# Decoder layer, attention stage: small vector operations placed in other quarters of a batch, the counting products in another quarter, and three places instead of two for stacked queries and keys

## What is computed

```python
    x = x + _L0_attn_ref(_layernorm(x, axis=-1), ...)
    x = x + _L0_xattn_ref(_layernorm(x, axis=-1), ctx_768, ...)
    x = x + _L0_ffn_ref(_layernorm(x, axis=-1), L0_ffn_Wr, L0_ffn_W1, L0_ffn_W2)
```

```python
        q = (query @ Wq + bq).reshape(B, Nq, H, D).transpose(0, 2, 1, 3)
        k = (key_value @ Wk + bk).reshape(B, Nkv, H, D).transpose(0, 2, 1, 3)
        v = (key_value @ Wv + bv).reshape(B, Nkv, H, D).transpose(0, 2, 1, 3)
        attn = jnp.einsum('bhqd,bhkd->bhqk', q, k) * scale
        attn = jnp.clip(attn, -CLAMP, CLAMP)
        attn = jax.nn.softmax(attn, axis=-1)
        x = jnp.einsum('bhqk,bhkd->bqhd', attn, v).reshape(B, Nq, Cq)
        return x @ Wo + bo
...
        logits = flat @ Wr.T
        weights, ids = jax.lax.top_k(logits, K)
        weights = jax.nn.softmax(weights, axis=-1)
```

## Time and profile before

| | |
|---|---|
| median of 3 runs | 1611.56 us (1610.73 to 1614.21) |
| the profiled execution, its own time | 1611.83 us |
| its span, first to last instruction | 1609.9 us |
| PE busy in the span | 1367.0 us (85%) |
| DVE busy | 1020.0 us (63%) |
| POOL busy | 786.4 us (49%) |
| ACT busy | 553.0 us (34%) |
| one batch of the attention stage | 22.14 us (28 batches, 560.43 to 1180.40) |
| busy between 900 and 1000 us | PE 90.86, DVE 81.26, POOL 71.31, ACT 48.74 us |
| granted TensorE clock, mean of the span | 0.953 |

### The profile page before, as it was taken

How to read it: one execution, slowest core, us unless ns; L and a number is a source line. 1 busy time by engine, 2 the same in 40 slices (tenths; PEclk the granted TensorE clock), 3 DMA queues, 4 the chain that set the end, 5 groups by cost and what they waited for, 6 DMA issues and landing times. The chain is left out here.

```text
span 1609.9 us, 31655 instructions
## 1 busy us (share of the span) xinstructions
PE 1367.0 (85%) x9914; PEld 947.0 (59%) x9915; DVE 1020.0 (63%) x2361; ACT 553.0 (34%) x1356; POOL 786.4 (49%) x1072
## 2 busy tenths in 40 slices
PE   4788778877746998999998899999986699999996
PEld 2455555545534666666666666666664366666664
DVE  2687987798741777888787888888875122222221
ACT  1333323323311345444354444444442112122221
POOL 3234643463343557766666666777664122222222
PEclk9999999999975899999899999999995799999999
DMA  4992000000005655656555564655551122222222
GB/s 148 304 321 60 1 1 1 0 0 1 1 0 92 93 85 106 117 113 107 109 103 115 109 113 96 111 117 118 112 110 38 39 45 44 46 46 46 44 45 23
DMA packets 180329, 128.01 MB, mean 80 GB/s; under 512 B 69010, under 2 KB 173090, under 8 KB 180194
## 3 DMA queue, kind: packets, MB, share of 16 engines
q1 hardware_dynamic: 167890, 112.23, 33.0%
q0 software_dynamic: 12304, 14.10, 5.8%
HBM read 36.10 MB, written 44.83 MB: 50 GB/s over the span
## 5 line engine op out<-in xcount | busy, mean ns | idle before, releaser
L1327 DVE TENSOR_REDUCE neg_raw<-bank_s 100x2 f32<-100x722 f32 x256 | 231.0, 902 | 97.4 <-PE bank_s L1536 86.5
L1220 ACT ACTIVATE prob<-bank_st 120x400 f32<-120x400 f32 (+1 forms) x384 | 166.3, 512 | 190.1 <-PE bank_st L1553 190.1
L1877 POOL DMA_INDIRECT out<-result,target x57 | 88.2, 1547 | 266.6 <-DVE result L1851 263.7
L1338 DVE TENSOR_SCALAR bank_st<-bank_st 120x400 f32<-120x400 f32 (+1 forms) x384 | 195.3, 570 | 0.2 <-issue 0.2
L748 PE MATMUL bank_l<-q_heads,k 128*100 128x192 f32 (+4 forms) x512 | 119.3, 372 | 65.4 <-DVE attn L562 52.2
L1075 POOL TENSOR_TENSOR neg_diag<-xident_b,neg_max 100x400 bf16<-100x400 bf16 x128 | 109.4, 855 | 124.7 <-DVE neg_max L1332 116.4
L1862 DVE TENSOR_TENSOR hidden<-silu,ebank_v 128x512 f32<-128x512 f32 x57 | 39.2, 688 | 196.7 <-PE ebank_v L1786 196.7
L1536 PE MATMUL bank_s<-k_st,q_st 96*100 96x361 bf16 x512 | 130.6, 337 | 35.0 <-DVE neg_raw L1327 21.4
L748 PEld LDWEIGHTS bank_l<-q_heads,k 128*100 128x100 f32 x512 | 79.0, 172 | 113.8 <-DVE attn L562 43.2
L396 ACT ACTIVATE q_heads<-q 32x192 f32<-32x192 f32 (+3 forms) x168 | 62.1, 370 | 224.4 <-DVE q L521 221.4
L1544 PEld LDWEIGHTS bank_st<-q_st,k_st 96*120 96x120 bf16 (+1 forms) x1536 | 109.9, 137 | 22.2 <-ACT prob L1220 10.9
(11 more groups left out here) (203 smaller groups left out, 2724.7 us busy)
## 6 DMA issues: line engine op xcount, KB each, us to landing
k_st<-k_part SPq DMA_DIRECT2D x384, 90.2 KB
slot_rows<-empty SPq DMA_DIRECT2D x9, 2967.0 KB, 26.3
q_st<-q_part SPq DMA_DIRECT2D x384, 25.0 KB
kv<-in_ctx_t SPq DMA_DIRECT2D x32, 270.8 KB
expert_w<-in_w SPq DMA_DIRECT2D x16, 512.0 KB, 4.1
rows<-slot_rows SPq DMA_DIRECT2D x57, 129.0 KB
residual<-in_w SPq DMA_DIRECT2D x16, 256.0 KB, 4.5
residual<-in_x SPq DMA_DIRECT2D x8, 400.0 KB
```

The costliest lines, as they stand in the source:

```text
L1220: act.activation(prob[0:KEYS[c], t % 2, c], bank_st[c][0:KEYS[c], 0:4 * T], ACT.Exp).then_inc(exp_done, 1)
L1327: dve.tensor_reduce(neg_raw[:, h:h + 2], bank_s[0:T, :, 0:S], AX.X, ALU.max, negate=True).then_inc(max_done, 1)
L1338: dve.tensor_scalar(tile, tile, CLAMP, -CLAMP, ALU.min, ALU.max).then_inc(clipped, 1)
```

## The change

Four things are altered in the attention stage.

1. `q_st` and `k_st` get a third place; batch b uses place b mod 3, and SP's `stack` waits for the score products of one batch less.
2. DVE: `moments(b + 2)` goes from quarter 1 to quarter 0, behind the clips. `norm(b + 2)` goes from quarter 1 to quarter 2, behind the clips. `moments3(b - 1)` goes from quarter 3, ahead of the clips, to quarter 2, behind them. `place` stays in quarter 0 of an even batch but comes behind max0 instead of ahead of it. `one_hots` stays in quarter 2 of an odd batch but comes last, behind `negated`, instead of ahead of `residual`.
3. PE: `count` goes from the end of quarter 3 of an odd batch to quarter 0 of the next batch, behind `scores_t`. `turn3` stays in quarter 0 but comes behind `scores` pair 1 and `weigh`.
4. In `tile_map`, after the last batch, two temporaries are dropped (their work goes into `past`) and the expert numbers are worked out ahead of the row numbers. The count of instructions is unchanged: 13.

The file becomes a few lines shorter, so that an operation at L1327 before stands at L1325 after, L1401 at L1399, L1607 at L1604.

```diff
-        q_st = sb("q_st", [96, 2, NH, T], BF16)
-        k_st = sb("k_st", [96, 2, NH, S], BF16)
+        q_st = sb("q_st", [96, 3, NH, T], BF16)
+        k_st = sb("k_st", [96, 3, NH, S], BF16)
...
-                until(st_summed, 12 * (b - 1))
-                until(s_summed, 8 * (b - 1))
+                until(st_summed, 12 * (b - 2))
+                until(s_summed, 8 * (b - 2))
...
-                    stack(b + 1, 1 - p)
+                    stack(b + 1, (b + 1) % 3)
...
                 for t in range(4):
                     n = 4 * b + t
                     go = t < 3 or more
-                    if t == 0 and p == 0 and not (isinstance(b, int) and b < 4):
-                        place(2 * i - 2 + q // 2, q // 2)
-                    if t == 1 and not (isinstance(b, int) and b < 2):
+                    if t == 1 and b >= 2:
                         best_two(b - 2, p, 2 * i - 1 + q // 2)
                     if go:
                         maxima(n + 1, (t + 1) % 4, 0)
-                    if more_than(b, 2) and t == 1:
-                        moments(b + 2)
-                    if t == 2 and p == 1 and not (isinstance(b, int) and b < 3):
-                        one_hots(2 * i - 1 + q // 2)
-                    if t == 2 and not first:
+                    if t == 0 and p == 0 and b >= 4:
+                        place(2 * i - 2 + q // 2, q // 2)
+                    if t == 2 and b:
                         residual(b - 1, 1 - p)
-                    if t == 3 and not first:
-                        moments3(b - 1)
                     for c in range(3):
                         clip(n, c)
-                    if t == 1 and not first:
+                    if t == 0 and more_than(b, 2):
+                        moments(b + 2)
+                    if t == 1 and b:
                         normalise(b - 1)
-                    if more_than(b, 2) and t == 1:
+                    if t == 2 and more_than(b, 2):
                         norm(b + 2)
-                    if t == 3 and not first:
+                    if t == 2 and b:
+                        moments3(b - 1)
+                    if t == 3 and b:
                         norm3(b - 1, (q - 1) % 4, i if q else i - 1)
                     if go:
                         maxima(n + 1, (t + 1) % 4, 1)
                         negated(n + 1, (t + 1) % 4)
+                    if t == 2 and p == 1 and b >= 3:
+                        one_hots(2 * i - 1 + q // 2)
...
                     for c in range(3):
-                        scores_t(n, p, t, c)
-                    if t == 0 and routed:
-                        if p == 0 and not (isinstance(b, int) and b < 4):
-                            pe.wait_ge(chosen_done, 2 * i - 1 + q // 2)
-                        if more:
-                            turn3(b - 2, (q - 2) % 4, k_done, CC * (b + 2))
...
+                        scores_t(n, b % 3, t, c)
+                    if t == 0 and p == 0 and b >= 4:
+                        count(2 * i - 2 + q // 2, k_done, CC * (b + 2))
```

50 lines of the change are left out of this document (24 added, 26 removed).

## The result

The changed kernel takes 1615.4 us (median of 13 runs, 1612.5 to 1621.8), the kernel before beside it on the same chip 1610.3 us (13 runs): a ratio of 1.0035, interval 1.0020 to 1.0051, or 5.1 us more. The profiled execution took 1621.34 us, with a span of 1619.4 and a mean granted clock of 0.945 (before 1611.83, 1609.9 and 0.953). Of these 9.5 us only part is the change. The mixer, where the code is the same, already took longer: the attention stage's first quarter starts at 529.38 us instead of 523.68, and over the fourteen profiled executions of this study that start lies anywhere from 523.7 to 530.7. The 28 batches from quarter 3 of batch 1 (566.08) to quarter 3 of batch 29 (1187.94) take 621.86 us, against 619.97 before; another 2 us came behind them. Each kernel has one traced execution, and that of the changed kernel is 5.9 us above its median.

The account below looks back on a forecast made before the run. PE leads, so its waits, mainly for DVE's `maxima` and the queries, decide. Quarter lengths sum to 629.2 us over 28 batches against 619.97 (+9.2), plus 0.5 elsewhere: 1611.8 + 9.7, so 1621 us; own range 1614 to 1629, wider 1595 to 1633.

Parts of the forecast that it names:

- its own signs: Right: quarter 2 at 5.2 to 5.3, no `q_st` wait, `norm3` at 1.4 us; wrong: PE still waiting for queries.
- Quarter 2: DVE's loop with the moved `norm` and `moments3` sets the quarter: 5.25 us, old mean about 4.85.
- Third place: Third place of `q_st` and `k_st`: costed at nothing, with 13.5 us as the upper bound of its gain.
- Quarter 3: `norm3` held by POOL, so the start of `kr` counts: 5.87 us in even batches (now 5.73), 5.7 in odd (now 5.89).
- Quarter 0 of even batches: `slots`, now behind max0, starts in the middle of POOL's `kr` and is held: 6.0 us, now 4.8.
- Quarter 1 of odd batches: `neg_max` held by POOL, by up to 1.1 us, makes max0 late and eats the gain: 6.4 us.
- The wait for the queries: Ahead of quarter 3: query DMAs land by 22.3 us, the batch is 22.3 to 22.6 long, so nothing added.
- quarter 1 of even ones: Starts late, with ACT's `exps` done and `heads` 0.66 us earlier: 5.7 us in place of 6.45.
- C: Rival: no change; old waits hide more of quarter 2 and `slots` is held briefly: 1612 us, chance 0.20.
- B: Rival: waits for queries (13.5 us) and `count` (10.8) go, moved DVE work is hidden: 1587.5 us, chance 0.08.
- A: Rival: DVE's `norm3` gets ahead of `kr` in quarter 3, then 4.8 to 4.9 us long: 1596 us, chance 0.10.
- D: Rival: `slots` held 2 us or more in each even batch, PE falls to its lower clock: 1639 us, chance 0.09.

Follow-up runs that it names:

- merged form: The two channel halves of each query part go in one DMA, 6 per batch in place of 12: kernel before 1601.7 us, changed kernel 1609.6 us.

## Why the prediction was right, and where its steps were not

Slower was right, and 1615.4 lies in the range and in the forecast's own range (1614 to 1629), 5.6 us under the 1621. In the 28 batches the sum was 629.2 and 621.86 was measured, so that the stretch which was to grow by 9.2 us grew by 1.9 in the traced pair, while the medians are 5.1 apart. That the total came so near is in part luck: two terms were too large by 10 us together, and waits that had been put at nothing gave some 3 back. Of its own signs, one of those for being wrong came up (PE waits for the queries still), `norm3` was not at 1.4 us, and there are more stretches at the lower clock than before. Point by point:

**Quarter 2: right.** 5.25 forecast, 5.12 in batches without another wait, 5.26 and 5.41 in the mean (the waits for the queries in odd batches make it 2 us more than forecast over the 28). The path on DVE was the one that was added up, 0.14 us shorter through overlap. In the merged form, where PE never waits for the queries, the old length is 4.16 and 4.61 and the new one 5.12: the old mean of 4.8 was partly a wait, as the prediction read it.

**Third place: right**, by the kernel that has it alone.

**Quarter 3: right in its result, wrong in a term.** 5.87 and 5.7 were forecast, 5.85 and 5.65 measured. In even batches `kr` began 3.08 us after the quarter did (3.15 forecast) and the quarter ended 2.71 later. The step that DVE "then follows" the middle part held, but `norm3` went from 1.40 to about 1.79 us, since it asks 0.04 us behind `kr` now and has to sit through both parts. The 5.65 of odd batches is a mean of 4.73 to 5.57 in eleven of them and of 6.29 to 7.79 in the three that ran in part at the lower clock, so there the agreement is chance.

**Quarter 0 of even batches: mis-sized by 5 us.** 6.0 was forecast and 5.87 is what a batch with the hold takes (`slots` 0.80 where 0.72 was assumed from batch 12). But in the even batches 4 to 28 `slots` took over half a microsecond in 8 of 13 only. In the other five it took 0.16 to 0.25 us and the quarter 5.2 to 5.3. Each of the five follows an odd batch whose quarter 3 began with a wait for the queries, and POOL stood later there. In batch 14, held, `kr` began 1.20 us after the quarter did and `slots` was asked for at 2.11. In batches 12 and 16 `kr` began at 2.08 and `slots` came just ahead of it; in batches 18, 20 and 22 `kr` was nearly over when `slots` asked. Such a wait doesn't always help: batches 8, 10 and 26 follow one too, `kr` had just begun or was half done there, and `slots` took 0.52 to 0.83. The mean of 5.56 in place of the 5.92 that the forecast comes to makes the sum 14 x 0.36, some 5 us, smaller. In the merged kernel, which has no such waits, all 13 `slots` from 600 to 1150 us were held (0.65 to 0.87).

**Quarter 1 of odd batches: mis-sized by another 5 us.** "It can be held, here by up to 1.1, which makes `best_two` and max0 late and eats the gain: 6.4." The measured length is 6.01, in nearly every one of them. `neg_max` in quarter 0 of batch 15 took 0.36 us, 0.2 more than unheld: it asked at 864.60 in the low part and ended at 864.96, right behind it (864.94), without waiting for the query part that POOL had begun at 864.89. The 1.1 us had been an upper bound for a hold by both; it was taken as the value, though no row bears it. 14 x 0.38 is 5.3 us. Of the 10 us that these two terms were too large, the longer quarters 2 of odd batches and quarter 1 of even ones (5.79 in place of 5.7) took 3 back, which leaves the 7.3.

**The wait for the queries: the step that failed.** "The wait for the queries does not add to it: their DMAs ... have landed by 22.3, and the new batch is 22.3 to 22.6 long." The batch from an even quarter 3 was 22.3 long only through the 6.4 above. Its own quarters came to 5.79 + 4.83 + 6.01 + 5.12 = 21.75, while the queries were there 22.16 us after that quarter 3 began (876.58 less 854.42). So eleven of the fourteen waits of the changed kernel fall on the start of quarter 3 of an odd batch. The forecast listed "no wait for `q_st` left" as the sign of being right, and PE waited 22.0 us.

**The clock: no term at all.** Waits in longer pieces were followed by stretches at a granted clock of 0.5 (0.51 from 741.4 to 748.2, behind 1.77 us). Against the merged form of the same kernel, queries and clock together cost the changed kernel 8.7 us in the 28 batches (621.86 less 613.19), and the kernel before 12.4 (619.97 less 607.62). Both pay it, so 8.7 us of it cancel. The other 3.7 went in favour of the changed kernel, and are why the 5.6 us that the moves cost in the merged form are only 1.9 in the pair as it stood. It doesn't cancel in the experiments: three of them became clearly slower than the kernel that they were made from, and a fourth no faster, although quarters of theirs became shorter.

**The rivals.** C (a brief hold of `slots`, old waits hiding part of quarter 2; 1612) is 3.4 us from the result, nearer than the forecast's 5.6, and half of its mechanism is there: the missing hold in five batches. B's 13.5 us for the queries did not come. A was 0.04 us away in batch 14. That a `norm3` which starts first is short was an estimate, with 0.40 as the shortest of the earlier trace rows; forced by a wait of POOL it took 401 to 415 ns, and there the quarter came out as stated and the total did not. D's 2 us hold occurred in no batch of the changed kernel, its lower clock in four stretches, though behind waits for the queries and not behind `slots`.

What stays open is why the queries' DMAs arrive so late in single batches. In batch 24 they landed 4.25 us after the last issue, where 1.53 is usual; `send` transfers were under way there, but no kernel ran that takes them away. Nor was it tried what makes a wait of 1.8 us cost the clock in one batch and not in another (none followed 1.80 us at 1100.51 and 1.53 at 697.51; 6.8 us of it followed 1.77 at 741.42, and 3.4 us 1.27 at 787.90; where `kr` waits for `norm3`, none followed even 2.69 us at 655.10). Where the 5.1 us between the medians lie is open too: the traced pair is 9.5 apart, of which 1.9 are in the 28 batches, 1.9 behind them and the rest in the mixer, where nothing was changed.

## What to carry to other kernels

Before you cost a gain, add up every path that ends at the same place, the one through the DMA queue included, and compare it with the length that the batch will have, not the one it has: an engine's gain stops at the next path. When PE's waits get longer, count the time at the lower clock behind them as well. When a path of small DMAs ends such a wait, merge the DMAs first; only then do moves on the other engines show what they are worth. And look where a DVE operation falls in POOL's chain: in this kernel `neg_max`, 0.17 us long, took 1.81 where it was asked for just ahead of `kr` (875.71 against 875.79) and 0.44 where it was asked for in the middle part.
